# A scan over time between two routed layers: VectorE multiplies one block in sixteen by C out of PSUM, delta*x gets a ring of four pairs, and TensorE spreads the maxima

## The reference, cut to what matters

```
ffn(x): vecs = A x            # 64 experts, 16 numbers each
        top 4 experts by the norm of their 16 numbers; routes = 1/4 for these, else 0
        v    = sum over experts of routes * vecs
        out  = W x + bias + sum over experts of routes * B_expert v
x = x + 0.5 * ffn(layernorm(x))
x = x + scan(layernorm(x)):   # D = 1024 channels, 16 states each
        delta_r, B, C = split(W_xproj x)
        delta = softplus(W_dt delta_r + b_dt);   dA = exp(delta * A)
        h_t = dA_t * h_(t-1) + delta_t * x_t * B_t
        y_t = sum over the 16 states of h_t * C_t ;   result y + x * D_param
x = x + 0.5 * ffn(layernorm(x))
```

## Time and profile before

| | |
|---|---|
| median of 3 executions | 2844.78 us (2843.44 to 2848.23) |
| the profiled execution itself | 2852.74 us |
| span of its profile | 2851.0 us |
| busy: TensorE, GpSimd, VectorE, ScalarE | 2604.9, 2347.1, 2189.6, 1448.4 us |
| DMA engines' mean busy share in the scan | about 0.48 |

### The profile page before, as it was taken

The page is one execution under the profiler, slowest core; times in us unless marked ns, Lnnn a source line. Parts: engine busy times, 40 slices in busy tenths (PEclk is TensorE's granted clock), DMA queues, the critical chain, the costliest instruction groups (busy, mean ns, idle before and its releaser), DMA issues.

```text
span 2851.0 us, 38123 instructions
## 1 busy us (share of the span) xinstructions
PE 2604.9 (91%) x13056; PEld 1158.5 (41%) x13120; DVE 2189.6 (77%) x2661; ACT 1448.4 (51%) x3075; POOL 2347.1 (82%) x703
## 2 busy tenths in 40 slices
PE   4998999999899999989999999999899989988999
PEld 1454444444333434334444343444334433433444
DVE  7434788788888878888888788888888888878533
ACT  5334565555555555545655465555555545454211
POOL 2103999899999999999899999999999999999300
PEclk8999999999999999999999999999999999999999
DMA  5125445554445444554454346444454455444221
GB/s 214 51 62 132 140 133 137 155 154 141 127 131 159 129 129 139 154 137 134 130 167 133 116 131 169 144 127 141 148 148 144 118 157 148 123 137 122 67 60 52
DMA packets 309368, 373.40 MB, mean 131 GB/s; under 512 B 148147, under 2 KB 224051, under 8 KB 309174
## 3 DMA queue, kind: packets, MB, share of 16 engines
q1 hardware_dynamic: 292278, 337.40, 40.7%
q10 hardware_dynamic: 16896, 33.56, 4.0%
HBM read 234.05 MB, written 103.29 MB: 118 GB/s over the span
## 4 chain that ended last, share of the span: by engine, by line
PE 22%; DVE 18%; POOL 10%; DMA 8%; issue 7%; DVEq 5%; ACT 4%; ACTq 1%; SPq 1%; POOLq 0%
DVE mreg L1062 9%; PE pv L491 7%; POOL mreg L459 5%; PE po L491 5%; PE pv L495 3%; POOL mreg L451 3%; DMA delta_scratch<-mreg 3%; PE po L495 3%; DMA mreg<-xnT_scratch 2%; PE py L651 2%; ACT pA L855 1%; POOL mreg L446 1%; DMA uT<-sel 1%; DVE pv L1029 1%; DVE sel L1026 1%
## 5 line engine op out<-in xcount | busy, mean ns | idle before, releaser
L459 POOL TENSOR_TENSOR mreg<-mreg 128x2048 f32<-128x2048 f32 x256 | 1161.1, 4536 | 20.9 <-ACT hst L844 20.7
L1062 DVE TENSOR_TENSOR_SCAN mreg<-pA,hst,mreg 128x512 f32<-128x512 f32 x768 | 940.1, 1267 | 75.5 <-ACT hst L844 45.5
L451 POOL TENSOR_TENSOR mreg<-mreg 128x1024 f32<-128x1024 f32 x340 | 795.8, 2365 | 234.9 <-DMA mreg<-delta_scratch 231.9
L855 ACT ACTIVATE pA<-mreg,nA 128x512 f32<-128x512 f32 x1024 | 696.7, 684 | 467.2 <-DVE mreg L1062 412.9
L491 PE MATMUL po<-wB,uT 128*128 128x512 f16 x2016 | 476.7, 386 | 30.3 <-DMA uT<-sel 16.9
L491 PE MATMUL pv<-wA,xT 128*128 128x512 f16 x2016 | 462.4, 383 | 39.6 <-ACT xT L769 30.5
L491 PE MATMUL po<-wW,xT 128*128 128x512 f16 x2016 | 467.0, 380 | 8.0 <-issue 7.0
L446 POOL TENSOR_TENSOR mreg<-mreg 128x2048 f32<-128x2048 f32 x86 | 390.7, 4544 | 1.6 <-issue 1.6
L1062 DVE TENSOR_TENSOR_SCAN mreg<-pA,cst,mreg 128x512 f32<-128x512 f32 x256 | 313.4, 1267 | 30.4 <-ACT hst L844 20.7
L491 PEld LDWEIGHTS pv<-wA,xT 128*128 128x128 f16 x2016 | 194.0, 99 | 320.6 <-ACT xT L769 76.6
L491 PEld LDWEIGHTS po<-wB,uT 128*128 128x128 f16 x2016 | 192.7, 99 | 321.9 <-issue 94.2
(11 more groups left out here) (132 smaller groups left out, 2346.9 us busy)
## 6 DMA issues: line engine op xcount, KB each, us to landing
mreg<-delta_scratch SPq DMA_DIRECT2D x256, 512.0 KB, 5.6
delta_scratch<-mreg ACTq DMA_DIRECT2D x128, 256.0 KB
xin<-x SPq DMA_DIRECT2D x32, 512.0 KB, 4.5
x_scratch<-xin SPq DMA_DIRECT2D x32, 512.0 KB, 7.2
xnT_scratch<-auxs SPq DMA_DIRECT2D x32, 512.0 KB, 2.9
mreg<-xnT_scratch SPq DMA_DIRECT2D x64, 256.0 KB, 6.4
mreg<-bc_scratch SPq DMA_DIRECT2D x64, 256.0 KB, 5.5
yT_scratch<-mreg SPq DMA_DIRECT2D x64, 256.0 KB, 2.4
```

The lines of the kernel that those rows point to most:

```text
L451: pool.tensor_tensor(Hr[:, G % NH, 2 * h:2 * h + 2, :], u, b.broadcast_to([P, 2, CT]), ALU.mult).then_inc(s_bm, 1)
L459: pool.tensor_tensor(h, h, Cr[:, g, :].unsqueeze(1).broadcast_to([P, 4, CT]), ALU.mult).then_inc(s_cm, 1)
L855: nc.scalar.activation(pA[:, i % 2, :], Dr[:, 2 * (n % NPR) + i % 2, :], ACT.Exp, scale=nA[:, c:c + 1]).then_inc(s_dA, 1)
L1062: V.tensor_tensor_scan(h, pA[:, i % 2, :], h, before, ALU.mult, ALU.add).then_inc(s_sc, 1)
```

## The change

Constants: `NPU = 4` is the new ring of delta*x pairs, `OWN = (3,)` the group of each tile whose last block VectorE multiplies itself. Block 3 of group 3 is one block in sixteen.

```diff
 def scan(i):                                   # VectorE
+    if s == 3 and G % 4 in OWN:
+        a = pA[:, i % 2, :]
+        V.tensor_tensor_scan(a, a, h, before, ALU.mult, ALU.add)
+        dve.drain()
+        dve.wait_ge(s_ldc[G % 4], 16 * (G // NG + 1))
+        V.tensor_tensor(h, a, Cr[:, G % 4, :], ALU.mult).then_inc(s_sc, 1)
+        return
     V.tensor_tensor_scan(h, pA[:, i % 2, :], h, before, ALU.mult, ALU.add).then_inc(s_sc, 1)

 def times_c(G):                                # GpSimd
+    n = 3 if g in OWN else 4
-    h = Hr[:, G % NH, :, :]
+    h = Hr[:, G % NH, 0:n, :]
 def times_b(G):                                # always the whole group now
-    if g in (1, 2) and pair[0] < pair[1]: ... one product of 128x2048
-    else: two products of 128x1024, each after its own pair has landed
+    pool.wait_ge(s_ldu[n], 32 * (t // (NPU // 2) + 1))
+    pool.tensor_tensor(Hr[:, G % NH, :, :], Ur[:, 4 * n:4 * n + 4, :], b, ALU.mult).then_inc(s_bm, 2)

 def keep_last(G):                              # ScalarE: 3 columns from Hr, the 4th from pA
 def decay(i):                                  # ScalarE: other groups keep their column after the decay, not ahead of it

 def load_dt(t):                                # SP: W_dt now comes in slices of 128 columns
+    sp.wait_ge(s_z, t)
+    sp.dma_start(wdt[:, :], WdtT[:, t % KD * P:(t % KD + 1) * P]).then_inc(s_ldw, 16)
 def slot(a, n):                                # SP
+    if G % 4 == 0 and t + 1 < NCH * KD:
+        load_dt(t + 1)
+    if G % 4 == 1 and t < NGRP // 4:
+        spread_inputs(t, 0)
+        spread_inputs(t, 1)
     if G % 4 == 2:
         if t >= 2:
             store_tile(t - 2)
         if t < NGRP // 4:
-            spread_inputs(t, 0)
-            spread_inputs(t, 1)
             spread_delta(t, 0)

 # start: the maxima are spread by TensorE and reduced by VectorE
-    pool.partition_all_reduce(amr[:, n:n + 1], amm[:, n:n + 1], P, RMAX).then_inc(s_amr, 1)
+    nc.tensor.matmul(py[:, n * P:(n + 1) * P], amm[:, n:n + 1].broadcast_to([P, P]), idf[:, :], ...)
+    V.tensor_reduce(amr[:, lo:hi], py[...], AX.X, ALU.max)          # both later maxima in one chain
```

More of the change, by code:

```diff
@@ L464, in _ @@
                 low(wA, k, stA[:, k, :]).then_inc(s_loAp, 1)
-            largest(2)
-            largest(1)
-            for k in range(KB, KD):
-                pool.wait_ge(s_scB, k + 1 - KB)
-                low(wB, k, stB[:, k, :] if k < NB5 else stB2[:, k - NB5, :]).then_inc(s_loBp, 1)
+            for k in range(NLW, KD):
+                pool.wait_ge(s_scW, k + 1 - NLW)
+                low(wW, k, stW[:, k, :]).then_inc(s_loWp, 1)
             times_b(0)
@@ L537, in first_base @@
             def first_base(a):
-                pe.wait_ge(s_bsc, 1)
-                for nb in range(2):
-                    nc.tensor.matmul(po[:, nb, :], onesb[:, :], brow[:, nb * HF:(nb + 1) * HF], start=True, stop=False)
                 for k in range(KD):
@@ L546, in first_base, with first_base_low @@
                             nc.tensor.matmul(po[:, nb, :], xT[:, part, k, :], wW[:, 0, k, nb * HF:(nb + 1) * HF],
-                                             start=False, stop=False)
+                                             start=(k == 0 and part == 0), stop=False)
+                pe.wait_ge(s_bsc, 1)
+                for nb in range(2):
+                    nc.tensor.matmul(po[:, nb, :], onesb[:, :], brow[:, nb * HF:(nb + 1) * HF], start=False, stop=False)
+            def first_base_low():
                 for k in range(KD):
-                    pe.wait_ge(s_loW, k + 1)
+                    if k < NLW:
+                        pe.wait_ge(s_loW, k + 1)
+                    else:
+                        pe.wait_ge(s_loWp, k + 1 - NLW)
                     for nb in range(2):
@@ L647, in states @@
                 pe.wait_ge(s_cm, G + 1)
+                if G == 0:
+                    pe.wait_ge(s_set, 1)
+                if g in OWN:
+                    pe.wait_ge(s_sc, 4 * G + 4)
                 if g == 0:
@@ L978, in low, with lows_w @@
                 return V.scalar_tensor_tensor(w[:, 1, k, :], src, sc[:, col:col + 1], w[:, 0, k, :], ALU.mult, ALU.subtract)
+            def lows_w(lo, hi):
+                for k in range(lo, hi):
+                    low(wW, k, stW[:, k, :], 2, s_hiW).then_inc(s_loW, 1)
             def stats(ln, src, s_done):
@@ L1087, in unit @@
                 if a.u == 0:
-                    for k in range(KB):
-                        low(wB, k, stB[:, k, :], 1, s_hiB).then_inc(s_loB, 1)
+                    lows_w(2, NLW)
+                    for k in range(KD):
+                        low(wB, k, stB[:, k, :] if k < NB5 else stB2[:, k - NB5, :], 1, s_hiB).then_inc(s_loB, 1)
                 scans(2, 5)
```

176 lines of the change are left out of this document (92 added, 84 removed).

## The result

| | before | after |
|---|---|---|
| median | 2846.26 us (4 runs) | 2898.83 us (4 runs, 2895.89 to 2901.96) |
| ratio | | 1.019, 95% interval 1.0177 to 1.0203 |
| profiled execution | 2852.74 us | 2895.89 us |
| unit 5 begins, by the same mark as in the earlier trace rows | 262.68 us | 260.15 us |
| unit 5 to unit 58 | 2398.45 us | 2444.10 us |

A forecast was written before the change was run, and what follows sets the result against it. GpSimd (96.4% busy) and TensorE (92.2%) were taken as near their limit, the sum made in TensorE's idle time. 2852.74 - 41 - 10 + 16 + 22 = 2839.7, as a median 2832 us; range 2792 to 2882.

The forecast's parts named there:

- The signs named for it: TensorE's GpSimd wait at most 15 us, xT and xn below 110; GpSimd busy near 2255, over 100 idle.
- the own product: VectorE's 64 products by C at 0.69 us, 44 us in all, partly hidden: +16 us, ends 0 and +44.
- SP's order: Delta*x loads moved up one slot on SP wait for s_std and delay later transfers: +22 us, ends 0 and +79.
- GpSimd's relief: GpSimd's products take 93 us less; TensorE gains only its wait for GpSimd: -41 us, ends 0 and -71.
- rival C: No change: TensorE's relief becomes a longer wait for xT, 10 of 41 us remain; 2846 us median, chance 0.14.
- the third only ahead of `low_part`, where VectorE waits for ScalarE: Own product in a unit's third slot: counted as covered, so only two of five slots cost.
- First place: Eleven tiles whose load falls in a unit's last slot: `load_x` 3 us late, 1.2 each taken, 13 us.
- Second place: Ten units with z at positions 0 and 1: `load_tile` 1.7 us late, 0.9 each taken, 9 us.
- the wait for z(t) in slot 0: SP's wait ahead of `load_x` in units with z at positions 0 and 1: given no size of its own.
- The start: Before unit 5: ScalarE starts on W earlier, low parts take 5.2 us less: -10 us, ends -4.7 and -12.
- Rival B: Slower: SP's waits delay `load_x`, `turn` and `load_tile`, +50 us, relief 35; 2866 us median, chance 0.33.
- D's product: Rival where VectorE's own product is never hidden: +44 instead of +16, 2860 us; no chance of its own.

The follow-up runs named there:

- e5: e1 with the load of the W_dt slice moved from a unit's first slot to its second; 2852.82 us, ratio 1.0027.
- e7: e5 without VectorE's own products, so GpSimd makes all four blocks of each group; 2844.18 us, ratio 0.999.
- e2: The changed kernel without VectorE's own products (`OWN = ()`), all else as changed; 2872.66 us, ratio 1.010.
- e8: e5 with the own product in the fifth slot of each unit that has five, 44 places instead of 64; 2829.13 us, ratio 0.9943.
- e10: The changed kernel, its SP order untouched, with the own products placed as in e8; 2871.63 us, ratio 1.0091.
- e9: e8 with its 44 own products in the second slot of the unit instead of the fifth; 2856.84 us, ratio 1.0037.
- e1: The changed kernel with the two loads of delta*x back in the third slot, behind the store of y; 2862.02 us, ratio 1.0055.
- e4: The changed kernel with the delta*x loads back behind the store of y only in units with z at positions 0 and 1; 2892.01 us, ratio 1.0168.
- e11: The changed kernel with only the load of the W_dt slice moved from a unit's first slot to its second; 2887.58 us, ratio 1.015.
- e3: The changed kernel with only the delta*x loads in a unit's last slot issued after the unit's own store of x; 2884.69 us, ratio 1.014.
- e6: The kernel before with only VectorE's own product added, and the decays ahead of ScalarE's copy that belong to it; 2855.73 us, ratio 1.0038.
- e12: e8 with own products also in the last slot of units with four slots, 53 places; 2832.8 us, ratio 0.9947.

## Why the prediction was wrong

The right steps were the durations, and GpSimd's busy time (2250.4 us in the whole span against 2255 worked out). The signs named for it came in part: the wait for GpSimd vanished, but xT and xn went to 123.5 us, over the 110 named, and GpSimd's idle time was not a sign of gain.

Two steps failed. The larger one is the own product with its relief: I had them at -41 + 16 = -25, and the runs have +10.5 with SP's order as before (e5 against e7, by the ratios) and +26 with it changed (after against e2). The smaller is SP's order: +22 forecast, 28 without own products (e2 less e7), 46 with the 64 of the change (after less e5). In my sum, +10.5 in place of -25 alone gives 22 us slower; 28 in place of 22 on SP alone would still have said faster, and 46 gives 11 slower. The two do not add up, so no single split of the loss is the true one. One way through the runs is 2845.8 for the kernel before, -2.8 (e7), +10.5 (e5 against e7) and +46 (after less e5), 2899.5 for 2898.8; it closes because each step starts where the last one ended, and proves nothing. The parts:

- **GpSimd's relief, -41.** By an estimate from e7 and e8, 44 covered products give 15 us, 0.34 each, or 22 for 64, where SP's order is good; in the changed order it is next to nothing (e10 equals e2). In e8 against e7 TensorE's wait for GpSimd falls by 44 us (83.3 to 39.6), and its waits for xn and xT rise by 19 (69.1 to 88.2). The reason I gave for the lower end, that the wait for xT in the same unit "only grows by as much", is what the rows show; I put it in rival C and gave it 0.14.
- **The own product, +16.** Uncovered they cost 28/44 = 0.63 each (e9 less e8). With 64 spread evenly the net is +10.5, so by the estimate above the cost is 32, or 0.5 each: four of five slots uncovered, and e5's wait for the squares agrees, which took in one fifth. I had counted two of five. The step "the third only ahead of `low_part`, where VectorE waits for ScalarE", and the cover of the fourth, are thus in doubt: VectorE's waits for the decays ahead of the scans are 77.6 us in e7, without own products, and 76.5 in e5, with them, so they took in nothing. No run has own products in the third slot alone, nor in the fourth of a unit with five.
- **SP's order, +22, measured +28 to +46.** The bounds (0 and 79) held it. First place: 13 forecast, 29 measured by the units of class A (e1). I had priced `load_x` at 3 us late and then taken 1.2 of it, on the thought that "a transfer that starts late meets an emptier queue". It is 4.7 late on average, not 3, and costs 2.6 a place. Second place: 9 forecast for the store of y, 5 measured (e1, e4), which is no more than a class moves by itself. What I left "inside the bound" and never priced, the wait for z(t) in slot 0, cost 9 to 11 us (e5, e11), as much as the places that I did price. And I let the store of y land in 2.4 us behind two loads of 512 KB, while the row of 2.4 came from a store without them: it took 4.7 in the median and 7.1 at the place shown.
- **The account itself.** I made the sum in TensorE's idle time, "what can be won or lost". Of the 45.7 us in the stretch 17 are idle time and 29 are busy time, for which the sum had no term (see below on the granted clock).
- **The start, -10.** The ring, the products and the start together gave 2 to 3. ScalarE did start 4.1 earlier, near my end of -4.7; the 5.2 of the low parts did not reach unit 5, which begins 2.5 earlier. Whether the ring or the whole products took something back was not tested.

Rival B came nearest, "slower, by SP's order", and its sign, the later `load_x`, is there. But it is only a part of the truth. Its 50 us on SP are met by the 46 with the own products as they are; without them SP's order costs 28, under the 35 from which B was to decide. Its time of 2866 is too early by 33, because it kept a relief of 35 us and an own product at 16; what is missing is C's relief that turns into other waits and D's product that is mostly not hidden. That its 50 and the 46 are close is in part luck, since its place by place figures (3 and 1.7 us) are not the measured ones. The sign named for it in TensorE's waits for xin or uT (over 30 us) tells nothing: they were 30.2 before and are 25.4 after, 39.4 with the new one for `yT_scratch`. The one in unit 15 (over 7 us) failed, 5.14.

The sum failed in its form as well. The two terms that speak against the change were taken below the middle of their bounds, and the relief at its row in full, though a wait of TensorE that goes is replaced by the next. In hindsight, half of the relief, and the other terms at the middle of their bounds, would have given 2852.74 - 20 - 8 + 22 + 40 = 2886.7, as a median 2879, and the right sign.

What stays open: how much of the changed kernel's loss is TensorE's clock in its own right. Its busy time in the stretch rose by 29 us, and that is what the added half-speed time (below) takes almost exactly. The half-speed time falls back to that of before as soon as the loads do (e1), so its cost is counted in SP's order here and was not tested by itself.

## What to carry to other kernels

A load moved ahead of a store in one queue cost twice here: by the wait that goes with it, and, as the landings suggest, by its bytes, behind which the store and everything that waits for its landing comes late. Price the landing of the store with those bytes ahead of it, and price every wait that a queue of fixed order gets, the small ones too. Work given from the busiest engine to the second was worth something only where that engine waits afterwards anyway, and only while others still wait for the busiest one: the same 44 instructions made the kernel 15 us faster than without them in one slot and 13 slower in another, and in the order where TensorE hardly waits for GpSimd they gained nothing in the best slot. Two changes made at once are priced together, not each against the kernel before.

## What the runs showed of the hardware that was not expected

**TensorE's granted clock is a part of the loss.** By windows of 5 us from 240 to 2700 us, TensorE ran at its lower level (1.2 GHz, granted clock 0.5) for 82 us before and 143 us after. At half speed work takes twice as long, so 61 us more at 0.5 is 30 us of work lost, and the busy time rose by 29. The others: 82 us (e1), 106 (e2), 130 (e3), 126 (e4), 88 (e5), 85 (e6), 68 (e7), 75 (e8), 102 (e9), 95 (e10), 150 (e11), 55 (e12). From 240 to 2700 us the clock fell 18 times before and 34 times after. Each fall comes behind a gap in TensorE's work, but not each gap brings one. Unit 15 after, windows of 2 us (columns as in the earlier trace rows):

```profile
734.00:736.00 2.00, 2.00 (x9) 0.72 (x9) 1.93 (x5) 0.95 (x6) 2.00 (x1) 1.00 0.25 98
736.00:738.00 2.00, 0.57 (x3) 0.08 (x1) 1.95 (x2) 1.74 (x6) 2.00 (x1) 1.00 0.26 100
738.00:740.00 2.00, 1.27 (x9) 1.21 (x10) 0.61 (x1) 2.00 (x5) 0.38 (x1) 0.83 0.05 20
740.00:742.00 2.00, 2.00 (x6) 0.72 (x5) 1.84 (x2) 2.00 (x5) 0.00 (x0) 0.50 0.73 180
742.00:744.00 2.00, 2.00 (x12) 0.46 (x10) 1.72 (x2) 1.85 (x4) 0.00 (x0) 0.81 0.85 238
...
748.00:750.00 2.00, 0.00 (x0) 0.00 (x0) 0.11 (x1) 0.69 (x1) 2.00 (x1) 1.00 0.85 254
750.00:752.00 2.00, 0.68 (x4) 0.35 (x5) 2.00 (x3) 0.00 (x0) 2.00 (x2) 1.00 0.48 166
```

TensorE worked 0.57 of 2 us from 736 on, and the clock was down by 740 and back by 744; between 740 and 742 it made six matmuls, where it made 9 in the full window from 734 on, at granted clock 1.00. The longer gap at 748 to 750 brought no fall. So a wait can cost more than its own length. That a kernel with more waits pays more by this is what the times above suggest, not shown by itself.

**A store's landing is later with loads ahead of it.** The same 256 KB took 2.4 us in the median before, and in e1, where the loads are back, 2.5; 4.7 after, and 7.1 behind three loads and another store.
